# Mixing stage of a two-layer convolution kernel: short h ring with stored and reloaded h, other tap split, layer norm's columns on GpSimd

## The reference

```
h   = gelu(batchnorm(conv1x1(haar(groupnorm(x)), w_c1) + b_c1))      # 128 channels
o   = dwconv3x3(h, dw_w) + dw_b
o   = layernorm over (channels, rows, columns) of each image, scale gn_g, shift gn_b
o   = gelu(conv1x1(o, pw1_w) + pw1_b)
u   = conv1x1(o, pw2_w) + pw2_b + h
x   = x + inverse_haar(gelu(batchnorm(conv1x1(u, w_c2) + b_c2)))
out = x + blur4x4(groupnorm(x))
```

## Time and profile before

| | |
|---|---|
| median of 3 runs | 5608.24 us (5605.93 to 5615.25) |
| the profiled execution's own time | 5612.93 us |
| its span in the trace | 5611.1 us |
| busy share of the span: TensorE, VectorE, ScalarE, GpSimd | 93%, 77%, 66%, 37% |
| mean bandwidth of all transfers | 308 GB/s |
| taps on VectorE (L699, into dw_psum) | 551.3 us busy, 753 ns each |
| product adds on GpSimd (L648) | 607.4 us busy, 1276 ns each |

### The profile page before, as it was taken

How to read it: one execution, slowest core, us unless ns; L and a number is a source line. 1 busy time by engine, 2 the same in 40 slices (tenths; PEclk the granted TensorE clock), 3 DMA queues, 4 the chain that set the end, 5 groups by cost and what they waited for, 6 DMA issues and landing times. The chain is left out here.

```text
span 5611.1 us, 67501 instructions
## 1 busy us (share of the span) xinstructions
PE 5223.0 (93%) x18280; PEld 3171.0 (57%) x18280; DVE 4318.1 (77%) x5293; ACT 3702.3 (66%) x4976; POOL 2095.5 (37%) x1393
## 2 busy tenths in 40 slices
PE   2888888899999999997699999999999999999999
PEld 1333333334555555563266666666666667667777
DVE  8555555418999999966988888888888888888833
ACT  0333333346777777756788788787887878878754
POOL 0000000017777777742333333333333333333354
PEclk9999999999999999999899999999999999999999
DMA  9999999942333333326999999999999999999986
GB/s 372 367 383 387 376 382 377 354 147 81 106 107 108 106 109 107 105 87 258 382 388 403 394 404 399 394 404 390 395 399 388 404 392 395 404 382 404 394 273 221
DMA packets 829589, 1729.80 MB, mean 308 GB/s; under 512 B 50064, under 2 KB 587152, under 8 KB 718608
## 3 DMA queue, kind: packets, MB, share of 16 engines
q1 hardware_dynamic: 485136, 1121.34, 53.8%
q10 hardware_dynamic: 344064, 604.05, 28.1%
HBM read 1050.95 MB, written 674.23 MB: 307 GB/s over the span
## 5 line engine op out<-in xcount | busy, mean ns | idle before, releaser
L1159 POOL TENSOR_TENSOR y_lo<-y_centred_tile,y_hi 128x1024 fp32r<-128x1024 f32 x512 | 1039.7, 2052 | 1721.1 <-ACT y_centred_tile L1509 1405.3
L1380 PE MATMUL blur_psum<-y_hi,band_hi 128*128 128x512 f32 x4096 | 1128.9, 417 | 8.8 <-DVE y_tile L1248 7.4
L1380 PE MATMUL blur_psum<-y_lo,band_hi 128*128 128x512 f32 x4096 | 1042.5, 396 | 7.5 <-POOL y_lo L1159 7.1
L1363 PE MATMUL conv_psum<-u_in,w_conv 128*128 128x512 f32 x2048 | 958.1, 610 | 84.2 <-DMA u_in<-u_scratch 36.1
L1380 PEld LDWEIGHTS blur_psum<-y_hi,band_hi 128*128 128x128 f32 x4096 | 765.8, 188 | 278.9 <-issue 100.6
L1380 PEld LDWEIGHTS blur_psum<-y_lo,band_hi 128*128 128x128 f32 x4096 | 769.7, 188 | 200.8 <-POOL y_lo L1159 16.5
L1220 DVE TENSOR_TENSOR pair_sums<-gelu_out,conv_psum 128x512 f32<-128x512 f32 x960 | 613.9, 683 | 308.3 <-ACT conv_psum L1471 308.0
L1248 DVE SCALAR_TENSOR_TENSOR y_tile<-blur_psum,rstd_all,y_tile 128x1024 f32<-128x1024 f32 x512 | 639.5, 1276 | 159.7 <-PE blur_psum L1380 152.2
L1471 ACT ACTIVATE gelu_out<-conv_psum,bn_shift,bn_scale 128x512 f32<-128x512 f32 x512 | 397.9, 777 | 522.0 <-PE conv_psum L1363 498.9
L1363 PEld LDWEIGHTS conv_psum<-u_in,w_conv 128*128 128x128 f32 x2048 | 393.8, 195 | 525.3 <-issue 384.2
L396 PE MATMUL z_psum<-x_resident,w_folded 128*128 128x512 f32 x1280 | 600.0, 624 | 28.0 <-ACT z_psum L425 19.1
(11 more groups left out here) (175 smaller groups left out, 5661.9 us busy)
## 6 DMA issues: line engine op xcount, KB each, us to landing
x_tile<-x SPq DMA_DIRECT2D x256, 1024.0 KB, 9.1
y_scratch<-x_tile ACTq DMA_DIRECT2D x256, 1024.0 KB, 7.7
y_tile<-y_scratch SPq DMA_DIRECT2D x512, 512.0 KB, 12.5
out<-y_tile ACTq DMA_DIRECT2D x512, 512.0 KB, 9.7
x_stream<-x SPq DMA_DIRECT2D x192, 1024.0 KB, 11.6
x_resident<-x SPq DMA_DIRECT2D x160, 1024.0 KB, 11.2
z_scratch<-z_tile ACTq DMA_DIRECT2D x256, 256.0 KB, 7.2
z_in<-z_scratch SPq DMA_DIRECT2D x256, 256.0 KB, 3.0
```

Of the source, the lines that this page charges most:

```text
L1159: nc.gpsimd.tensor_tensor(y_lo[:, h, part, 2:2 + W], y_c[:, part, :], y_hi[:, h, part, 2:2 + W].bitcast(F32), ALU.subtract).then_inc(s_lo, 1)
L1363: nc.tensor.matmul(cv[s][:], w[:, s * C:(s + 1) * C], u_t[:, k % US, :], start=True, stop=True).then_inc(s_mm, 1)
L1380: ins = nc.tensor.matmul(bl[t][:, 2 * c:2 * c + 2, :], wt[:, kw, :], y[:, h, ch:ch + 2, kw:kw + W], start=(m == 0 and kw == 0), stop=(m == ...
```

## The change

- **h ring.** `h_ring` shrinks from 41 blocks to 8. SP stores each h block to DRAM (over the z it was made from) and loads it back into `h_in`, a new buffer of four slots, for `residual`. A writer of a ring block waits for its readers (`s_oo`) and for its store (`s_hst`), where it waited for `residual` before.
- **Split.** All steps have 2 taps on TensorE, 4 on VectorE and 3 on ScalarE, where the first 36 had 4, 3, 2. The product buffer is 2 x 3 slots. (The change goes by a name that also speaks of 12 slots and of a split 1, 4, 4 in turn with 2, 4, 3; the diff holds neither.)
- **Norm.** `norm_fold` leaves VectorE. GpSimd makes scale and shift (three operations on one column, behind its pow), and ScalarE scales the weights, at j = 6 between `gelu_second` and `gelu_first`.
- **Small things.** Three columns get tensors of their own, and `quarter` is filled in the mixing stage instead of the last.

```diff
-ENTER_TAPS = (4, 3, 2)
-STEADY_TAPS = (2, 4, 3)
-PE_MOST = 4
-PR_SLOTS = 6
+PE_TAPS = 2
+ACT_TAPS = 3
+DVE_TAPS = TAPS - PE_TAPS - ACT_TAPS
...
-BLOCKS = STEPS + 1 + BEHIND + 1
+BLOCKS = 8
+H_SLOTS = 4
...
-    return ENTER_TAPS if e < LEAVE - LAG_DW else STEADY_TAPS
...
-        diag = sb("tap_diagonals", [128, PE_MOST, C])
+        diag = sb("tap_diagonals", [128, PE_TAPS, C])
-        products = sb("tap_products", [128, PR_SLOTS, BANK])
+        products = sb("tap_products", [128, 2, ACT_TAPS, BANK])
...
+        def last_reader(at):
+            b, j = divmod(at, STEPS + 1)
+            return b * STEPS + min(j + 1, STEPS - 1) if j < STEPS else min((b + 1) * STEPS, ALL2 - 1)
+        def wait_place(engine, at):
+            if at == BLOCKS - 1:
+                engine.wait_ge(s_oo, 1)
             if at < BLOCKS:
-                return None
+                return
+            engine.wait_ge(s_oo, last_reader(at - BLOCKS) + 1)
             b, j = divmod(at - BLOCKS, STEPS + 1)
-            return b * STEPS + min(j, STEPS - 1)
+            if j < STEPS:
+                e = b * STEPS + j
+                engine.wait_ge(s_hst[e % 4], 16 * (e // 4 + 1))
...
+            def store_h(e):
+                sp.wait_ge(s_h, e + 1)
+                if e >= 4:
+                    sp.wait_ge(s_hst[e % 4], 16 * (e // 4))
+                b, j = divmod(e, STEPS)
+                sp.dma_start(zv[b, :, j * BANK:(j + 1) * BANK].rearrange("c (r w) -> c r w", w=W2),
+                             rows_of(e)).then_inc(s_hst[e % 4], 16)
+            def load_h(l):
+                if l >= H_SLOTS:
+                    sp.wait_ge(s_u, l - H_SLOTS + 1)
+                sp.wait_ge(s_hst[l % 4], 16 * (l // 4 + 1))
+                b, j = divmod(l, STEPS)
+                sp.dma_start(h_in[:, l % H_SLOTS, :], zv[b, :, j * BANK:(j + 1) * BANK]).then_inc(s_hin[l % H_SLOTS], 16)
...
-                if p >= LEAVE:
-                    store(p - LEAVE)
+                if 0 <= p - 1 < ALL2:
+                    store_h(p - 1)
+                if 0 <= p + 3 - LEAVE < ALL2:
+                    load_h(p + 3 - LEAVE)
+                if p - 1 >= LEAVE:
+                    store(p - 1 - LEAVE)
...
+            pool.memset(kp["quarter"][:], 1.0 / GRP).then_inc(s_zero, 1)
...
+            def norm_scale(b):
+                pool.wait_ge(s_pow, b + 2)
+                nc.gpsimd.tensor_tensor(t[:, 3:4], t[:, 2:3], neg_half[:, 0:1], ALU.pow).then_inc(s_rs, 1)
+                pool.wait_ge(s_rs, b + 2)
+                if b >= 1:
+                    pool.wait_ge(s_lnb, b)
+                    pool.wait_ge(s_ln, b)
+                nc.gpsimd.tensor_tensor(t[:, 6:7], t[:, 3:4], V[:, V_GNG:V_GNG + 1], ALU.mult).then_inc(s_sc, 1)
+                pool.wait_ge(s_sc, b + 1)
+                pool.wait_ge(s_dev, b + 1)
+                nc.gpsimd.tensor_tensor(t[:, 7:8], t[:, 8:9], t[:, 6:7], ALU.mult).then_inc(s_lkp, 1)
+                pool.wait_ge(s_lkp, b + 1)
+                nc.gpsimd.tensor_tensor(t[:, 7:8], t[:, 7:8], V[:, V_GNB:V_GNB + 1], ALU.add).then_inc(s_lnc, 1)
...
             def residual(l):
                 dve.wait_ge(s_p2, l + 1)
+                dve.wait_ge(s_hin[l % H_SLOTS], 16 * (l // H_SLOTS + 1))
...
-                    rows_of(l), ALU.add, ALU.add).then_inc(s_u, 1)
+                                               h_in[:, l % H_SLOTS, :], ALU.add, ALU.add).then_inc(s_u, 1)
...
-            def norm_fold(b):
-                dve.wait_ge(s_rs, b + 2)
-                ln.link(nc.vector.tensor_tensor(t[:, 6:7], t[:, 3:4], V[:, V_GNG:V_GNG + 1], ALU.mult))
-                ln.link(nc.vector.tensor_scalar(w1f[:, b % 2, :], w1[:], t[:, 6:7], None, ALU.mult))
-                nc.vector.scalar_tensor_tensor(t[:, 7:8], t[:, 8:9], t[:, 6:7], V[:, V_GNB:V_GNB + 1],
-                                               ALU.mult, ALU.add).then_inc(s_ln, 1)
...
+            def fold_weights(b):
+                if b == 0:
+                    act.wait_ge(s_w, 48)
+                act.wait_ge(s_sc, b + 1)
+                if b >= 2:
+                    act.wait_ge(s_p1, (b - 1) * STEPS)
+                nc.scalar.activation(w1f[:, b % 2, :], w1[:], ACT.Copy, scale=t[:, 6:7]).then_inc(s_ln, 1)
...
             for p in range(LAG_Z, ALL2 + LEAVE + LAG_EVAC):
                 l = p - LEAVE
+                b, j = divmod(p, STEPS)
                 if 0 <= l < ALL2:
                     gelu_second(l)
+                if j == LAG_STATS + 1 and 1 <= b <= B:
+                    fold_weights(b - 1)
```

More of the change, by code:

```diff
@@ L97, in build @@
         n128 = sbk("mean_over_channels", [128, 128])
+        quarter = sbk("quarter", [128, 128])
         gram = sbk("gram", [128, C + 1])
@@ L473 @@
 Z_SLOTS = 3
[L475 to L482, removed]
 def phase_mix(nc, kp, pw1, pw2, const, z_d, u_d):
@@ L531, in phase_mix @@
         s_h = sem("h_rows_ready")
+        s_hst = [sem(f"h_stored{i}") for i in range(4)]
+        s_hin = [sem(f"h_loaded{i}") for i in range(H_SLOTS)]
         s_dw = sem("dw_psum_ready")
@@ L598, in store @@
                 sp.dma_start(uv[b, :, j * BANK:(j + 1) * BANK], u_t[:, l % 4, :]).then_inc(s_ust[l % 4], 16)
-            for p in range(-AHEAD, ALL2 + LEAVE):
+            for p in range(-AHEAD, ALL2 + LEAVE + 1):
                 if p + AHEAD < ALL2:
@@ L695, in depthwise @@
                 acc = dw_p[e % 2][:]
-                on_pe, on_dve, _ = split_of(e)
-                for n, k in enumerate(range(on_pe, on_pe + on_dve)):
-                    to = o_buf[:, e % O_SLOTS, :] if n == on_dve - 1 else acc
+                for n, k in enumerate(range(PE_TAPS, PE_TAPS + DVE_TAPS)):
+                    to = o_buf[:, e % O_SLOTS, :] if n == DVE_TAPS - 1 else acc
                     taps.link(nc.vector.scalar_tensor_tensor(
@@ L778, in _ @@
                     depthwise(p - LAG_TAPS)
-                if j == LAG_STATS and 1 <= b <= B:
-                    norm_fold(b - 1)
                 if 0 <= p - LAG_STATS < ALL2:
@@ L800, in taps_step @@
                 if e >= 2:
-                    pe.wait_ge(s_lk_tap, DVE_BEFORE[e - 1])
-                count = split_of(e)[0]
-                for k in range(count):
+                    pe.wait_ge(s_lk_tap, (e - 1) * DVE_TAPS)
+                for k in range(PE_TAPS):
                     ins = nc.tensor.matmul(dw_p[e % 2][:], diag[:, k, :], tap(k, e),
-                                           start=(k == 0), stop=(k == count - 1))
+                                           start=(k == 0), stop=(k == PE_TAPS - 1))
                 ins.then_inc(s_dw, 1)
@@ L873, in gelu_first @@
                 at = block_of(e)
-                last = freed_by(at)
-                if last is not None:
-                    act.wait_ge(s_u, last + 1)
+                wait_place(act, at)
                 rows = z_in[:, e % Z_SLOTS, :].rearrange("p (r c) -> p r c", c=W2)
@@ L906, in tap_products @@
                 wait_rows(act, e)
-                for n in range(split_of(e)[2]):
-                    i = ACT_BEFORE[e] + n
-                    if i >= PR_SLOTS:
-                        e0, n0 = PRODUCTS[i - PR_SLOTS]
-                        if n0 == 0:
-                            act.wait_ge(s_oo, e0 + 1)
-                        else:
-                            act.wait_ge(s_add, ADD_BEFORE[e0] + n0)
-                    k = TAPS - split_of(e)[2] + n
-                    nc.scalar.activation(products[:, i % PR_SLOTS, :].rearrange("p (r c) -> p r c", c=W2), tap(k, e),
+                if e >= 2:
+                    act.wait_ge(s_oo, e - 1)
+                for n in range(ACT_TAPS):
+                    k = TAPS - ACT_TAPS + n
+                    nc.scalar.activation(products[:, e % 2, n, :].rearrange("p (r c) -> p r c", c=W2), tap(k, e),
                                          ACT.Copy, scale=V[:, V_DWW + k:V_DWW + k + 1]).then_inc(s_pr, 1)
@@ L1141, in _ @@
                     pool.memset(y[:, :, :, cols].bitcast(F32), 0.0).then_inc(s_set, 1)
-            pool.memset(quarter[:], 1.0 / GRP).then_inc(s_set, 1)
             for y in (seam_hi, seam_lo):
```

72 lines of the change are left out of this document (36 added, 36 removed).

## The result

The changed kernel takes 5601.16 us in the median of 20 runs (5595.27 to 5611.92), the kernel before 5609.71 in 20 runs beside them: ratio 0.9985, 95% interval 0.9978 to 0.9992, so 4 to 12 us faster. The forecast was 5607, with a range of 5588 to 5627. The profiled execution took 5602.11 us, its span is 5600.3.

The account below looks back on a forecast made before the run. TensorE was taken to bound the mixing stage, VectorE close behind, with GpSimd bounding the first 36 steps after the change. +16.1 - 3.2 - 13.8 + 0.3 = -0.6 on the 5608.24 us median, rounded to 5607; range 5588 to 5627.

Parts of the forecast that it names:

- no effect of the ring: Mixing stage: shorter ring, h store and reload cost nothing; transfers need 50 of 76 us of engine time a step.
- First 36 steps: Start of the mixing stage: GpSimd becomes the bound, 3.99 against 3.43 us a step; +16.1 us (bounds +11.6, +19.6).
- First image's norm: From step 32's final add to the first pw2: 9.9 instead of 14.6 us; with additions, -3.2 us (bounds -4.7, -1).
- Next six images: Image beginnings: pw1's 2.73 us wait goes, a 1.4 us wait of pw2 replaces it; -13.8 us (bounds -20, -5).
- My sentence on sensitivity: GpSimd's norm columns: an operation far from 0.4 us changes the total by 18 us for each us.
- B: Image beginnings: wait nearly vanishes, columns at 0.15 us, no lower clock, GpSimd's first-part step 3.85; faster, 5595 us; 18%.
- A: Whole kernel: the forecast as summed, two terms that cancel; 5596 to 5619 us by itself; 50%.
- C: First part: GpSimd's step is longer than its rows; at 4.5 us a step +16 us, 5624; 17%.
- D: Middle steps: transfers don't fit past 76 ns a small packet; at 89 ns +87 us, 5695; 10%.
- E: Middle steps: the change has a 1,4,4 split in turn, 0.07 us less over 217 steps; -15 us, 5592; 5%.
- four terms: Mixing stage: first 36 steps +16.1, first image's norm -3.2, next six images -13.8, last image's norm +0.3 us.

Follow-up runs that it names:

- split_only: The kernel before with only the first 36 steps changed from 4, 3, 2 to 2, 4, 3 taps; 5617.03 us, ratio 1.0020.
- norm_only: The kernel before with only the norm moved: scale and shift columns on GpSimd, weights scaled by ScalarE; 5578.44 us, ratio 0.9951.
- cols_more: The changed kernel with four more column operations on GpSimd in front of its adds; 5608.62 us, ratio 1.0001 to the kernel before.
- store_twice: The changed kernel with the first 36 steps back at 4, 3, 2 taps and each h block stored a second time; 5581.45 us, ratio 0.9948.
- cols_8: The changed kernel with eight more column operations on GpSimd in front of its adds; 5621.41 us, ratio 1.0017.

## Why the prediction was right, and where it was off

- **The shape held.** Two opposite terms, GpSimd as the bound of the first part, the pw1 wait gone, a shorter wait of pw2 for ScalarE's second GELU in its place, no effect of the ring: each was seen where it was forecast, and each has an experiment that shows it alone.
- **First 36 steps:** +16.1 forecast, +17.2 measured (18.6 - 1.4). The step of 3.99 us was met in 31 of 32 steps. One step is 0.6 us longer by GpSimd's zero rows, which the forecast left out, and step 0's final add came 0.4 us later than forecast after the stage's start. The lower clock that the forecast called free if it came did come, and was free.
- **First image's norm:** -3.2 forecast, -2.9 measured (3.9 less, 0.9 more until the next). The size is near by errors that offset each other, and that is luck. Step 33's final add was forecast 5.95 us behind step 32's and came after 6.80. The columns were 0.6 cheaper, but the variance wasn't ready "before GpSimd gets to it": VectorE's L759 ended 5.2 us after the start of the statistics (1362.69 to 1367.86) instead of 3.3, and GpSimd started its pow 1.4 us later than forecast. I had read the 3.3 in the kernel before, where GpSimd was idle while VectorE made these columns; in the changed kernel it was adding, and two of VectorE's column operations took 2.07 us instead of 0.38 (see below). The lower clock did come, after a pause of 6.12 us, but not on the way to pw2, so the 1.2 that I added for it stood for nothing. The 0.9 us until the next norm, 0.3 in the forecast, is the split's: `split_only` has it too, `norm_only` doesn't.
- **Next six images, the step that was mis-sized:** -13.8 forecast, -21.4 measured (16.4 + 5.0), past the -20 that I gave as the bound. Three things went into it. A GpSimd column operation takes 0.19 us and 0.08 for the hand-over, not 0.4 + 0.08, so the wait was 0.72, not 1.4: 6 x 0.68 = 4.1. The lower clock that I still charged with 0.3 an image never came: 1.8. And I took the cost of an image's beginning from five pitches, 5.4 us; the sixth interval, which I left out, had the lower clock too, and gave 5.0 instead of 3.3: 1.7. Together 7.6, which is the difference. I had put the unknown operation between VectorE's 0.15 and pow's 0.55, a little to the pow's side; at 0.19 a multiply of one column on GpSimd is near VectorE's end. The estimate of 0.3 that the prediction gives beside it lay nearer, and was still too high.
- **My sentence on sensitivity** (18 us of total for each us of a column operation) was of the right size, and a little low: it counts six images, and the first one pays too. `cols_more` adds 4 x 0.27 at seven images, +7.8 in the stage against 7.6.
- **Rivals.** B, faster because the wait nearly vanishes, came in part: the columns at 0.19 and no lower clock, as it said, but the first part was not shorter than its rows. The result lies between A and B. C and D didn't occur: the step of the first part is 3.99, and `store_twice` shows the transfers' room. E didn't either: six slots and one split are what the instructions show.
- **Small slips of the sum.** 5608.24 - 0.6 is 5607.6, which rounds to 5608, not 5607. The 0.72 from the second GELU to pw2 isn't in the earlier trace rows, where pw2 waits for TensorE; it is the GELU's 0.67 and a hand-over of 0.05, and the runs show 0.72.

By the stage the four terms come to -6.7 instead of -0.6, nearly all of it in the third. The median of the whole kernel moved by -8.5 where -0.6 was forecast; the range holds it.

## What to carry to other kernels

A small chain of column operations in front of a queue that others wait for costs its full length at every unit of work: here 1.08 us more of it was 1.08 us more of TensorE's wait. Move it to an engine that waits anyway, and check what stands behind it there; the best place that was tried here was ScalarE. When you take the time of a small operation from a trace, look at what the other engines did beside it, and whether they will do so after the change. A change that bundles parts should be timed in parts: here one was worth -26 us in the stage, one +14 to +18, one close to nothing, and the sum was -7.

## What the runs showed of the hardware

**Pause and clock.** The lower TensorE clock of the kernel before followed pauses of 2.73 us, at some images and not at others. At the later images, pauses of 0.72 us (changed kernel) and 1.80 us (`cols_more`) were never followed by it, and of the six pauses of 2.87 to 2.97 us in `cols_8` one was. At the first norm it followed the pause of 6.12 us. In the changed kernel's first part TensorE is 56% busy with pauses of at most 2.04 us between 1250 and 1340 us, and yet the lower clock came three times, each time after several steps with a pause of 2.04; the granted clock of that window is 0.91. So the length of the last pause alone doesn't tell it. The Trainium skill ("TensorE: Matmul & The Clock Gate", Part 1) says that the gate has two levels and goes to the lower one after the engine was idle for long enough; that the same pause has either result, and that the clock falls in a stretch of short pauses too, is what the runs here add with their numbers.

**VectorE beside GpSimd.** Two of VectorE's column operations at the changed kernel's first norm:

```profile
1364.48 0.77 DVE L749 TENSOR_TENSOR small_columns<-o_mean_var,vectors 128x1 f32<-128x1 f32 x1
...
1365.28 1.30 DVE L750 SCALAR_TENSOR_TENSOR small_columns<-small_columns,o_mean_var 128x1 f32<-128x1 f32 x1
```

GpSimd at that time:

```profile
1362.54 2.68 POOL L685 TENSOR_TENSOR tap_products<-tap_products 128x512 f32<-128x512 f32 x2
...
1365.31 1.26 POOL L689 TENSOR_TENSOR depthwise_out<-depthwise_out,tap_products 128x512 f32<-128x512 f32 x1
```

The same two lines at the second norm, where GpSimd is idle:

```profile
1520.18 0.16 DVE L749 TENSOR_TENSOR small_columns<-o_mean_var,vectors 128x1 f32<-128x1 f32 x1
...
1520.38 0.22 DVE L750 SCALAR_TENSOR_TENSOR small_columns<-small_columns,o_mean_var 128x1 f32<-128x1 f32 x1
```

A tensor_tensor of one column takes 0.77 instead of 0.16 us, a scalar_tensor_tensor 1.30 instead of 0.22, while GpSimd adds. Both end when the add beside them ends: at 1365.25 and 1366.58, the adds at 1365.22 and 1366.57. The taps, which read PSUM and one SBUF tile, take 0.75 in either case. The fold of the kernel before stood beside GpSimd's adds in the same way. Its 128x128 scaling took 1.26 and its last operation 1.12, and at the last image, where GpSimd doesn't add, 0.29 and 0.22. The last operation at the second image's norm, then the scaling at the last one:

```profile
1517.60 1.12 DVE L733 SCALAR_TENSOR_TENSOR small_columns<-small_columns,vectors 128x1 f32<-128x1 f32 x1
...
2460.15 0.29 DVE L732 TENSOR_SCALAR pw_folded<-pw_weights,small_columns 128x128 f32<-128x128 f32 x1
```

By these rows 1.9 of the 2.73 us that pw1 waited are this slowing, (1.26 - 0.29) + (1.12 - 0.22), an estimate; the rest would be the fold's place behind VectorE's taps. The Trainium skill ("GPSIMD Engine Reference", Key points) says that GpSimd shares SBUF interfaces with VectorE and contends with its instructions that have two SBUF inputs or run in a 2-port mode; these rows agree with it. No run here tests the reason apart, such as the fold on VectorE with GpSimd idle at every image.

**Packets.** The h store's 512 B pieces: in the changed kernel the queue is busy 73.2% of 76.3 us of engine time a step, 55.9, of which three large transfers take 37.2 (one and a half times the 32.5% that two took before): 18.7 / 512 = 36 ns a piece. The second store of `store_twice` adds (93.8% - 73.2%) x 76.3 = 15.7, 31 ns a piece. I had taken 30.
